# A fused vision transformer kernel: the remainder subtraction of GpSimd moved between the 8th and 9th scatter, ScalarE's rounding of 4 pieces at the head of the step, its rounding of 6 pieces in halves

## What is computed

```python
patches = X.reshape(B, C, N_PATCHES, PATCH, N_PATCHES, PATCH)
patches = patches.transpose(0, 2, 4, 1, 3, 5).reshape(B, N_PATCHES * N_PATCHES, IN_D)   # IN_D = 2352
tokens = jnp.einsum('bpi,hi->bph', patches, W) + b
...
h = h + _L0_attn_ref(_layernorm(h, axis=-1), ...)
h = h + _L0_ffn_ref(_layernorm(h, axis=-1), ...)
h = h + _L1_attn_ref(_layernorm(h, axis=-1), L1_attn_k)
h = h + _L1_ffn_ref(_layernorm(h, axis=-1), ...)
```

## Time and profile before

| what | value |
|---|---|
| median of 3 runs | 1111.09 us (1110.81 to 1112.61) |
| the profiled execution's own time | 1112.54 us |
| its span, first to last instruction | 1110.8 us |
| TensorE busy over the span | 921.6 us (83%) |
| VectorE busy | 861.9 us (78%) |
| GpSimd busy | 676.9 us (61%) |
| ScalarE busy | 500.6 us (45%) |
| mean granted TensorE clock | 0.897 of full speed |

### The profile page before, as it was taken

One profiled execution on the slowest core, in us unless ns is written; L12 is line 12 of the kernel. 1 busy time (PEld: TensorE's weight loads), 2 busy tenths in 40 slices (PEclk: granted clock), 3 DMA queues, 4 the chain that ended last, 5 costly groups with the idle time before them and its releaser, 6 DMA issues.

```text
span 1110.8 us, 21766 instructions
## 1 busy us (share of the span) xinstructions
PE 921.6 (83%) x6072; PEld 776.4 (70%) x6072; DVE 861.9 (78%) x3342; ACT 500.6 (45%) x1340; POOL 676.9 (61%) x622
## 2 busy tenths in 40 slices
PE   6999999999999995467675876776739998999992
PEld 2576666777767664366674866666639998999992
DVE  0488889888898985557677899999767776888883
ACT  1345555555544442111112454666526565666651
POOL 1016666667766643577777667777777554555652
PEclk9999999999999996578887888787759999999997
DMA  9856666556666104277779883765295988889886
GB/s 372 329 209 213 205 224 221 195 199 204 226 218 224 45 24 138 79 206 212 213 219 305 276 273 108 243 227 174 78 314 176 290 277 266 282 292 325 300 271 228
DMA packets 118665, 246.58 MB, mean 222 GB/s; under 512 B 20914, under 2 KB 85936, under 8 KB 112400
## 3 DMA queue, kind: packets, MB, share of 16 engines
q1 hardware_dynamic: 77440, 191.26, 51.6%
q0 software_dynamic: 18592, 34.68, 9.2%
q10 hardware_dynamic: 22512, 19.25, 5.6%
HBM read 201.68 MB, written 45.43 MB: 222 GB/s over the span
## 4 chain that ended last, share of the span: by engine, by line
PE 45%; DVE 24%; issue 9%; DMA 8%; SPq 7%; ACT 6%; ACTq 1%; DVEq 0%; POOL 0%; POOLq 0%
PE ps L971 10%; PE ps L949 7%; PE ps L750 4%; PE ps L817 3%; DMA xin<-lists_L 3%; PE ps L801 3%; SPq L604 2%; SPq L606 2%; SPq L597 2%; PE ps L1050 2%; PE ps L774 2%; ACT x_hi L1132 2%; PE ps L743 2%; PE ps L789 2%; DVE idx L1614 2%
## 5 line engine op out<-in xcount | busy, mean ns | idle before, releaser
L2093 POOL DMA_INDIRECT lists_L<-rows,slots x250 | 282.0, 1128 | 174.5 <-issue 173.6
L2121 POOL DMA_INDIRECT results_L<-xin x145 | 146.0, 1007 | 105.5 <-DVE xin L1893 73.9
L2121 POOL DMA_INDIRECT results_L<-xin,place x146 | 144.4, 989 | 58.4 <-issue 38.8
L750 PE MATMUL ps<-xin,w_emb 128*128 128x512 f32 x292 | 138.9, 612 | 10.5 <-DMA w_emb<-in_w_main 8.4
L971 PE MATMUL ps<-xin,QK 128*128 128x128 f32 x838 | 115.8, 290 | 2.2 <-DVE xin L1893 2.1
L971 PEld LDWEIGHTS ps<-xin,QK 128*128 128x128 f32 x838 | 108.3, 205 | 4.1 <-issue 4.0
L1293 ACT ACTIVATE QK<-ps,xin 128x256 f32<-128x256 f32 x164 | 64.3, 475 | 80.7 <-PE ps L949 80.7
L2102 POOL TENSOR_TENSOR x_lo<-xin,x_hi 128x2048 fp32r<-128x2048 f32 x13 | 60.3, 4635 | 65.3 <-ACT x_hi L1140 65.0
L750 PEld LDWEIGHTS ps<-xin,w_emb 128*128 128x128 f32 x292 | 53.1, 195 | 60.4 <-issue 49.0
L926 PE MATMUL ps<-ident,xin 128*128 128x128 f32 x291 | 65.2, 306 | 35.3 <-DMA xin<-lists_L 34.4
L1867 DVE TENSOR_SCALAR xin<-xin 128x128 f32<-128x128 f32 x291 | 91.8, 359 | 0.6
(11 more groups left out here) (312 smaller groups left out, 2430.4 us busy)
## 6 DMA issues: line engine op xcount, KB each, us to landing
xin<-in_x_main SPq DMA_DIRECT2D x48, 1536.0 KB, 6.8
xin<-in_w_L SPq DMA_DIRECT2D x81, 578.0 KB
xin<-in_w_L SPq DMA_DIRECT2D x98, 128.0 KB
xin<-lists_L SPq DMA_DIRECT2D x64, 132.0 KB
xin<-in_w_L ACTq DMA_DIRECT2D x65, 128.0 KB
x_hi<-results_L SPq DMA_DIRECT2D x13, 640.0 KB, 7.2
xin<-in_difference SPq DMA_DIRECT2D x13, 640.0 KB
xin<-in_distance SPq DMA_DIRECT2D x13, 640.0 KB
```

The lines of the kernel that those rows point to most:

```text
L750: mm = pe.matmul(psE[h], w_emb[:, k, :], xin[h][c][:, n, :], start=(k == 0), stop=False, skip_group_check=True)
L2093: pool.indirect_dma_start(out=lists[l.name], out_offset=bass.IndirectOffsetOnAxis(ap=slots_of(l, g, h)[:, t, k:k + 1], axis=0), in_=buf[:, ...
L2121: pool.indirect_dma_start(out=results[l.name], out_offset=bass.IndirectOffsetOnAxis(ap=where, axis=0), in_=yblk[u][:, q, :], in_offset=Non ...
```

## The change

Three things are moved or cut, all in the 16 steps.

ScalarE: `high0` of group g + 3 goes from behind the routing copies to the head of step g, ahead of the copy to `atok`. `high` is cut into `high_begin` (the first three of six pieces) at its old place and `high_end` (the other three pieces and the rest) behind `a2`.

VectorE: `low` subtracts the six pieces in two instructions of three, the second behind a wait of its own.

GpSimd: `low0` no longer stands ahead of the group's ten scatters. The first one, of group 3, comes ahead of all groups; then `low0` of group g + 4 stands between the eighth and the ninth scatter of group g, behind a new wait for `split`, which VectorE raises at the end of `low` of group g + 3.

```diff
-            def high(g, h, j):
+            def high_begin(g, h, j):
...
-                act.activation(x_hi[:, :, :].rearrange("p k n -> p (k n)"),
-                               xin[h][SPLIT][:, :, :].rearrange("p k n -> p (k n)"), ACT.Copy)
+                high_of(h, 0, KC // 2).then_inc(x_hi_ready, 1)
+
+            def high_end(g, h, j):
+
+                high_of(h, KC // 2, KC)
                 act.activation(rest[half[h], :], xrest[h][:, :], ACT.Copy).then_inc(x_hi_ready, 1)
...
             def front_step(g, h, j, ahead, ahead_e=True):
                 o, jo = 1 - h, j + h
+                if FIRST <= g + 3 < GROUPS:
+                    high0(g + 3, 1 - h, (g + 3) // 2)
                 if ahead:
                     a1(g + 1, o, jo)
                 b2(g, h, j)
...
                 if ahead_e:
-                    high(g + 2, h, j + 1)
+                    high_begin(g + 2, h, j + 1)
                 if ahead:
                     a2(g + 1, o, jo)
+                if ahead_e:
+                    high_end(g + 2, h, j + 1)
+                if ahead:
                     a3(g + 1, o, jo)
                 r1_x2T(L0, g, h, j)
                 r1_rows1(L0, g, h, j)
-                if FIRST <= g + 3 < GROUPS:
-                    high0(g + 3, 1 - h, (g + 3) // 2)
...
             def low(g, h, j):
-                dve.wait_ge(x_hi_ready, g)
+                dve.wait_ge(x_hi_ready, 2 * g - 1)
...
+                for part_, (first, end) in enumerate(((0, KC // 2), (KC // 2, KC))):
+                    if part_ == 1:
+                        dve.wait_ge(x_hi_ready, 2 * g)
...
-            def low_and_send(g, h, j):
-                if g + 3 < GROUPS:
-                    low0(g + 3, 1 - h)
-                send(L0, g, h)
-
-            pairs(pool, low_and_send)
+            def send_and_low(g, h, j):
+                send(L0, g, h, 0, 8)
+                if g + 4 < GROUPS:
+                    pool.wait_ge(split, g + 4)
+                    low0(g + 4, h)
+                send(L0, g, h, 8, TILES * TOP)
+
+            low0(FIRST, FIRST % 2)
+            pairs(pool, send_and_low)
```

More of the change, by code:

```diff
@@ L1123, in _, with high_of @@
             act.dma_start(per_row[:, :], a["per_row"].to_broadcast([128, D + L1.E + 1])).then_inc(consts_in, 16)
-            def high(g, h, j):
+            def high_of(h, first, end):
+                return act.activation(x_hi[:, first:end, :].rearrange("p k n -> p (k n)"),
+                                      xin[h][SPLIT][:, first:end, :].rearrange("p k n -> p (k n)"), ACT.Copy)
+            def high_begin(g, h, j):
                 act.wait_ge(chunk_in[h][SPLIT], 32 * (j + 1))
@@ L1257, in _ @@
             guess(LNA, 0, statsA, logA, guessA)
-            high(1, 1, 0)
+            high_begin(1, 1, 0)
+            high_end(1, 1, 0)
             for f in (a2, a3, a4):
@@ L1442, in low @@
             def low(g, h, j):
-                dve.wait_ge(x_hi_ready, g)
-                x = xin[h][SPLIT][:, :, :].rearrange("p k n -> p (k n)")
+                dve.wait_ge(x_hi_ready, 2 * g - 1)
                 if g == 1:
@@ L1449, in low @@
                                           w_rest_hi[half[of], :].bitcast(F32), ALU.subtract)
-                dve.tensor_tensor(x_lo[:, :, :].rearrange("p k n -> p (k n)"), x,
-                                  x_hi[:, :, :].rearrange("p k n -> p (k n)").bitcast(F32), ALU.subtract)
+                for part_, (first, end) in enumerate(((0, KC // 2), (KC // 2, KC))):
+                    if part_ == 1:
+                        dve.wait_ge(x_hi_ready, 2 * g)
+                    dve.tensor_tensor(x_lo[:, first:end, :].rearrange("p k n -> p (k n)"),
+                                      xin[h][SPLIT][:, first:end, :].rearrange("p k n -> p (k n)"),
+                                      x_hi[:, first:end, :].rearrange("p k n -> p (k n)").bitcast(F32), ALU.subtract)
                 dve.tensor_tensor(rest[half[1 - h], :], xrest[h][:, :], rest[half[h], :].bitcast(F32),
```

## The result

The changed kernel takes **1195.02 us** (median, 1193.53 to 1197.77) and the kernel before, beside it on the same chip, 1111.03 us (1110.81 to 1112.61): ratio 1.0764 [1.0741, 1.0787]. It is slower by 84 us. 1202 us had been forecast, with a range of 1173 to 1222.

The account below looks back on a forecast made before the run. TensorE was taken to bound the embedding stage, idling only 0.44 us a step. 13 x (5.3 gap + 2.0 clock - 0.3 gain) = 91 us on the median 1111.09 gave 1202 us, range 1173 to 1222.

Parts of the forecast that it names:

- Part 1, the gap: ScalarE's head copy waits for tile 5, delaying atok and ntok; TensorE idles and each of 13 steps grows 5.3 us.
- Part 2, the clock: After the gap TensorE runs at a lower clock, costing 2.0 us a step, bounded between 0 and 3.4.
- bounds of rows 8: Lower-clock stretches read from the profile before: 3.4 us after a 2.15 us gap, 6.9 us after 4.35 us idling.
- Parts 3 and 4, the gain: GpSimd's moved subtraction shortens oh and the halves free XT: together at most 0.3 us back a step.
- `V` beside the subtraction: VectorE's V now runs beside GpSimd's subtraction; taken as not held, 0 us, with 2.0 us as upper bound.
- `oh` at 0.56 us: Sign in the changed trace: VectorE's oh pair, freed of GpSimd's subtraction, takes 0.56 us where it took 2.48.
- The clock that holds: Rival: TensorE's clock does not fall after the gap, 13 x (5.3 - 0.3) = 65 us, 1176 us; chance 0.13.
- The longer stretch: Rival: the clock stays low longer, 6.9 us with half lost, 109 us more, 1220 us; chance 0.13.
- `V` held: Rival: GpSimd's subtraction holds VectorE's V, 2.0 us more a step, 117 us in all, 1228 us; chance 0.04.
- The wait that is met a step earlier: Rival: group g + 1's tile 5 meets the copy's wait, so only gains of at most 6 us stay, 1105; chance 0.04.

Follow-up runs that it names:

- filled gap: The changed kernel with five spare 128x512 TensorE products between tile 8 and the ntok transposes, keeping TensorE busy while it waits: 1167.11 us, ratio 1.0505.
- three pieces: The changed kernel with three pieces of chunk 0 rounded and split instead of four, still one buffer: 1182.65 us, ratio 1.0668.
- wait alone: The kernel before with only the copy's wait for tile 5 put at ScalarE's head, the copy itself at its old place: 1175.76 us, ratio 1.061.
- move and halves: The changed kernel with ScalarE's four-piece copy back at its old place, GpSimd's moved subtraction and the halves kept: 1103.44 us, then 1100.80 us when run again.
- two-buffer kernel: The changed kernel with three pieces copied at ScalarE's head and two buffers for them, used in turn by even and odd groups: 1100.80 us, ratio 0.9918.
- copy alone: The kernel before with only the four-piece copy and its two waits moved to ScalarE's head: 1211.75 us, ratio 1.0916.
- copy between the guesses: The changed kernel with the four-piece copy moved behind guessA and ahead of guessB, one buffer: 1103.76 us, ratio 0.9937.

## Why the prediction was right

**Part 1, the gap: 5.3 us forecast, 5.0 measured.** Every link held. The copy waits for tile 5 of its own step; `bnA` starts 224.60 - 222.00 = 2.60 us behind it, where it started 2.79 us ahead of it: 5.4 late, as worked out. From `bnA` to `ntok` it is 3.69 us instead of 3.95, and `ntok` itself takes 1.37 instead of 1.50. I had counted 0.16 of these 0.39 us.

**Part 2, the clock: 2.0 forecast, 2.1 by the filled gap.** The mean is right, the picture too simple. It isn't one stretch per step but three in turn. Two other steps of the changed kernel, TensorE's timeline and the clock at the ends of its lower level:

```profile
165.38 1.13 PE L774 MATMUL ps<-ident,ntok 104*128 104x104 f32 x5 [5.17 <-DVE ntok L1500]
198.02 1.13 PE L774 MATMUL ps<-ident,ntok 104*128 104x104 f32 x5 [5.16 <-DVE ntok L1500]
...
164.00:165.00 1.00, 0.00 (x0) 0.00 (x0) 1.00 (x5) 1.00 (x2) 0.00 (x0) 0.91 0.30 93
171.00:172.00 1.00, 1.00 (x4) 0.80 (x3) 0.66 (x1) 0.27 (x1) 0.26 (x1) 0.68 0.00 0
...
195.50:196.50 1.00, 0.00 (x0) 0.00 (x0) 0.79 (x9) 0.32 (x2) 0.65 (x1) 0.52 0.87 344
201.50:202.50 1.00, 1.00 (x3) 0.45 (x2) 1.00 (x2) 0.18 (x1) 0.00 (x0) 0.57 0.00 0
```

In the first the clock falls at 164.8 and rises at 171.6, in the second it falls at 195.5, still inside the gap, and rises at 202.4: 6.8 us each. Of that TensorE works through 6.3, 4.3 and, in the step shown further up, 3.4 us; half of their mean is 2.3 us a step, and the filled gap says 2.1 to 2.3. The stage's granted clock reads 0.91 and not 0.94, as part of the lower level lies in the gap. The bounds of rows 8 (3.4 and 6.9 us) were thus both there, in turn.

That the value between them came out is in part luck. The second row didn't show what I read from it: in the kernel before, the clock had been at 1.2 GHz since 411.6 us, ahead of that gap of 4.35 us, so the gap didn't bring it down. And the cost doesn't follow the length of the gap: 4.73 us cost 1.4 us of clock (three pieces), 3.35 cost 3.0 (wait alone), 5.17 cost 2.3. Between 55 and 425 us of these three runs every stretch at the lower level lasts 3.4 or 6.8 us; what decides which of them follows a gap stays open.

The Trainium skill (TensorE: Matmul & The Clock Gate, section "HAM oscillation — how this bites in real kernels") has a loop where each turn starts at the lower clock, 1.67 us of it a turn. The trace of the changed kernel agrees that each turn pays, but with 3.4 to 6.8 us; by the page's figure the sum would have been 1187 us, and 1195 were measured.

**Parts 3 and 4, the gain: 0.3 forecast as the most, 0.78 measured.** This is the term that failed. I bounded it by TensorE's idling in the step, 0.44 us. But idle time understates TensorE's waits: in its timeline a product is often shown as running on past the start of the next one, so that a short wait behind it shows little or nothing. Before, from L750 at 190.89 to Q at 192.89 it is 2.00 us, of which 0.10 is idle; in the kernel with move and halves:

```profile
187.51 1.90 PE L750 MATMUL ps<-xin,w_emb 128*128 128x512 f32 x4
189.25 1.04 PE L789 MATMUL ps<-XT,small 128*128 128x260 f32 x4
```

Here it is 1.74, and Q starts 0.16 us ahead of the shown end of the products before it (187.51 + 1.90 = 189.41): before, Q waited 0.26 us for `XT` (which ended at 192.24 + 0.61 = 192.85), without a bracket. From `r3` (179.24) to the attention product (181.47) it was 2.23 us, and is 1.81 now (176.35 to 178.16): 0.42, where the bracket showed 0.26. In front of `r3` it is 0.17. Not every wait is in every step: from the `ntok` transposes to Q it was 2.51 and 2.25 us in turn, and the 0.17 is in the other steps. From `ntok` to `ntok` the two steps from 165.06 to 215.74 were 25.32 and 25.36 us long, 24.57 and 24.58 in the kernel with move and halves. So 13 x 0.48 = 6 us of the 7 that the forecast lay too high are here, and 13 x 0.3 = 4 in the gap; the clock takes 1 to 4 back.

`V` beside the subtraction was taken as not held: 1.22 us as before, while GpSimd subtracts from 236.07 to 240.68. `oh` at 0.56 us came as forecast too.

**The rivals.** The clock that holds (1176) fell with the clock row. The longer stretch (1220) came in two steps of three, but begins inside the gap, 0.6 and 2.5 us ahead of its end. `V` held fell. The wait that is met a step earlier was given 1105: it fell with the wait for tile 5, but the two-buffer kernel has made just that, with three pieces, and took 1100.8.

**The sum.** 13 x (5.0 + 2.1 - 0.78) = 82 us, with the 2.3 of the periods 85; measured 84.

## What to carry to other kernels

When an instruction moves up on an in-order engine, price its wait and not its length: read from another queue's wait on the same semaphore when it is raised, and see who is queued behind. A buffer shared from step to step turns a harmless early copy into a 5 us hole, and a second buffer gives it back. And bound a gain by start-to-start times of the engine that sets the pace, not by its idle time alone.

## What the runs showed of the hardware that I had not expected

- GpSimd's TENSOR_TENSOR holds VectorE's TENSOR_SCALAR as well as its `oh`: `rows` took 6.46 us beside it instead of 1.37 (copy alone) and `ntok` 5.56 (copy between the guesses, first step), while `V`, which reads PSUM, took its usual 1.22 (changed kernel). The Trainium skill (SBUF — State Buffer, section "Who interferes with whom") says that a VectorE tensor_scalar can, where its operands allow it, take the pair of ports that VectorE shares with GpSimd and so contend with it, and that a VectorE instruction with at most one SBUF input, outside the modes that use both ports, does not; `rows` and `V` agree.
- It goes the other way too. Before, a scatter of GpSimd that lies beside VectorE's x_lo subtraction (192.35 to 195.70) takes three times as long as its neighbours:

```profile
191.91 1.00 POOL L2093 DMA_INDIRECT lists_L<-rows,slots  x1 [0.30 <-issue]
193.21 3.36 POOL L2093 DMA_INDIRECT lists_L<-rows,slots  x1 [0.30 <-issue]
```

  The long one ends at 196.57, 0.16 us behind VectorE's next subtraction, the rest (195.72 + 0.69 = 196.41); in all 13 steps that have such a scatter it ends 0.15 to 0.18 us behind the rest. In the changed kernel the first eight scatters are over before VectorE subtracts, and each takes 1.00 us.
- What a gap costs in clock doesn't go by its length: in steady steps 3.35 us cost 3.0 us (wait alone), 4.73 cost 1.4 (three pieces) and 5.17 cost 2.3 (changed kernel), and one gap of 3.31 us left the clock at 1.00.
